# A message-passing layer with a mixture of experts: each quad of the edge stage in three steps, and indices by one transfer per three groups

## What is computed

```python
def gnn(node_feats, ...):
    neigh = segment_sum(node_feats[src], dst, num_segments=n)     # over 200000 edges
    h = (1.0 + eps) * node_feats + neigh
    h = relu(h @ W1 + b1) @ W2 + b2                                # 256 -> 512 -> 256
    return (h - h.mean(0)) * rsqrt(h.var(0) + 1e-5) * gamma + beta # over all nodes

x = x + gnn(layernorm(x), ...)
x = x + ffn(layernorm(x))   # softmax gate, best of 8 experts, capacity 1954 nodes each, 256 -> 1024 -> 256
```

## Time and profile before

| | |
|---|---|
| Timed runs, median of 3 | 2559.24 us (2556.51 to 2567.18) |
| Profiled execution, span | 3175.1 us |
| PE busy | 1826.2 us (58%) |
| DVE busy | 1442.5 us (45%) |
| ACT busy | 694.9 us (22%) |
| POOL busy | 1710.4 us (54%) |
| First to last gather transfer | 118.0 to 2285.7 us |
| Mean granted TensorE clock | 0.777 |

### The profile page before, as it was taken

One profiled execution on the slowest core, in us unless ns is written; L12 is line 12 of the kernel. 1 busy time (PEld: TensorE's weight loads), 2 busy tenths in 40 slices (PEclk: granted clock), 3 DMA queues, 4 the chain that ended last, 5 costly groups with the idle time before them and its releaser, 6 DMA issues. The chain is left out here.

```text
span 3175.1 us, 32785 instructions
## 1 busy us (share of the span) xinstructions
PE 1826.2 (58%) x9046; PEld 1097.7 (35%) x9047; DVE 1442.5 (45%) x4225; ACT 694.9 (22%) x1116; POOL 1710.4 (54%) x1690
## 2 busy tenths in 40 slices
PE   0154444455545455655554455564568768989995
PEld 0022212222222222322222222232357645566664
DVE  8765511543225422531252112122336557786885
ACT  6600000000010001000100001110046554636642
POOL 0366664655645565555644444445315556767874
PEclk9976667676767677777877777777776688999997
DMA  7533354324633354234423332212246432222220
GB/s 244 188 104 106 116 184 138 106 88 132 197 101 91 115 182 148 87 121 144 152 65 121 120 111 65 67 54 79 54 145 216 131 93 75 71 84 73 79 83 18
DMA packets 201521, 361.08 MB, mean 114 GB/s; under 512 B 62117, under 2 KB 125947, under 8 KB 201334
## 3 DMA queue, kind: packets, MB, share of 16 engines
q0 software_dynamic: 69152, 185.00, 19.3%
q1 hardware_dynamic: 130038, 172.60, 16.8%
q10 hardware_dynamic: 2144, 1.05, 0.1%
HBM read 291.08 MB, written 71.92 MB: 114 GB/s over the span
## 5 line engine op out<-in xcount | busy, mean ns | idle before, releaser
L791 POOL DMA_INDIRECT halves<-table,halves x1240 | 1187.7, 958 | 1011.5 <-issue 367.1
L879 PE MATMUL e_sums<-halves 128*128 128x256 f16 x1920 | 334.7, 346 | 392.8 <-issue 244.1
L1062 DVE SCALAR_TENSOR_TENSOR nodes<-e_sums,above,nodes 128x256 f32 (+1 forms) x161 | 77.3, 480 | 967.0 <-remote 437.4
L879 PEld LDWEIGHTS e_sums<-halves 128*128 128x128 f16 x1920 | 229.6, 122 | 508.3 <-issue 425.7
L936 PE MATMUL e_up<-e_hT,W1s 128*128 128x512 f32 (+1 forms) x400 | 229.8, 734 | 234.9 <-ACT e_hT L985 140.2
L985 ACT ACTIVATE e_hT<-e_up 128x1024 f32<-128x1024 f32 (+1 forms) x25 | 25.2, 1007 | 1524.0 <-remote 1185.3
L1720 POOL TENSOR_TENSOR x_midl<-x_midf,x_midh 128x512 f16<-128x512 f32 x200 | 298.7, 1517 | 104.9 <-ACT x_midh L1854 99.4
L917 PE MATMUL e_tally<-w1f,counts 128*128 128x512 f16 x490 | 165.5, 480 | 281.6 <-DMA w1f<-table 204.9
L1126 DVE TENSOR_TENSOR counts<-counts,e_tally 128x490 f32 x220 | 159.8, 726 | 267.8 <-PE e_tally L907 147.9
L1810 PE MATMUL x_down<-halves,x_midh 128*128 128x256 f16 x1472 | 249.4, 277 | 16.6 <-DVE x_yb L1947 15.0
L1786 PE MATMUL x_up<-x_xTh,halves 128*128 128x512 f16 (+1 forms) x800 | 233.6, 371 | 3.1 <-ACT x_midh L1854 3.1
(11 more groups left out here) (208 smaller groups left out, 2752.4 us busy)
## 6 DMA issues: line engine op xcount, KB each, us to landing
w1f<-table SPq DMA_DIRECT2D x120, 512.0 KB
halves<-table,halves POOLq DMA_INDIRECT x1240
slot_rows<-halves SPq DMA_DIRECT2D x64, 268.0 KB
x_row<-slot_rows SPq DMA_DIRECT2D x32, 536.0 KB, 7.4
table<-halves SPq DMA_DIRECT2D x25, 512.0 KB, 2.9
counts<-in_x SPq DMA_DIRECT2D x24, 512.0 KB, 4.5
r_xin<-in_x SPq DMA_DIRECT2D x24, 512.0 KB
out<-r_row SPq DMA_DIRECT2D x24, 512.0 KB
```

Source lines behind the costliest of these rows:

```text
L791: pool.indirect_dma_start(got[:, r, t, :], None, table.rearrange("p h d -> (p h) d"), bass.IndirectOffsetOnAxis(ap=idx[:, r, t:t + 1], axi ...
L879: ins = nc.tensor.matmul(sums[:, place, 0:D], hot[:, place, t, :], got[:, r, t, half * D:(half + 1) * D], start=(t == 0 and half == 0), st ...
```

## The change

Each quad is divided into three steps: the transposes with ACT's copy, the product with W1 with the relus, and the product with W2 with the results. They stand behind three successive groups. A quad starts at its place in `AT`, or where the quad ahead of it has ended: quads 0, 18, 1, 20 and 21 start one or two steps later than before. DVE's measuring comes four steps after the start. In place of its own wait for the results ahead of it, DVE's copy to `hrow` waits until the quad before is through W1, which guards the memory that `hrow` shares with `hT`. The last quad stays whole, behind what is left of quad 23.

The row numbers of an iteration's three groups come by one transfer of 96 bytes per partition, into one of two buffers in turn. Iterations 0 and 1 are loaded at the start. Iteration n+2 is loaded when the three groups of iteration n have landed, behind the pieces of iteration n. POOL waits for indices once per iteration, and its two loops now hold two iterations in their bodies.

The core of the diff:

```diff
+TURN_AT, UP_AT, DOWN_AT, MEASURE_AT = {}, {}, {}, {}
+_slot = 0
+for _q in ORDER[:-1]:
+    _slot = max(_slot, AT[_q][0] * RG + AT[_q][1])
+    TURN_AT[_slot], UP_AT[_slot + 1], DOWN_AT[_slot + 2], MEASURE_AT[_slot + 4] = _q, _q, _q, _q
+    _slot += 3
+STEPS = NIT * RG
+LATE = range(STEPS, max(MEASURE_AT) + 1)
...
-        idx = halves.lend(I32, RG, GT)
+        idx = halves.lend(I32, 2, RG * GT)
...
-                def indices(n, r):
-                    first = n * (RG * GT) + (HT + r * GT)
-                    sp.dma_start(idx[:, r, :], rows_of[:, bass.ds(first, GT)]).then_inc(s_idx[r], 16)
-
-                for r in range(RG):
-                    indices(0, r)
+                def indices(n):
+                    first, width = HT + n * RG * GT, min(RG, NG - n * RG) * GT
+                    sp.dma_start(idx[:, n % 2, 0:width], rows_of[:, first:first + width]).then_inc(s_idx[n % 2], 16)
+
+                indices(0)
+                indices(1)
...
-                def next_indices(n, r):
-                    sp.wait_ge(s_got[r], n * (16 * GT) + 16 * GT)
-                    indices(n + 1, r)
...
                     for r in range(RG):
                         for number in pieces_at(n, r):
                             piece(number)
-                        if (n + 1) * RG + r < NG:
-                            next_indices(n, r)
+                    if n + 2 < NIT:
+                        for r in range(RG):
+                            sp.wait_ge(s_got[r], (n + 1) * (16 * GT))
+                        indices(n + 2)
...
-                with pool.Fori(0, SINGLE // RG):
-                    for r in range(RG):
-                        pool.wait_ge(s_idx[r], have)
-                        pool.wait_ge(s_sum, done)
-                        pool.reg_add(done, done, 1)
-                        gather(r)
-                    pool.reg_add(have, have, 16)
+                with pool.Fori(0, SINGLE // RG // 2):
+                    for h in (1, 0):
+                        pool.wait_ge(s_idx[h], have[h])
+                        pool.reg_add(have[h], have[h], 16)
+                        for r in range(RG):
+                            pool.wait_ge(s_sum, done)
+                            pool.reg_add(done, done, 1)
+                            gather(h, r)
...
                     ins.then_inc(s_turn, 1)
+
+                def product_up(q, width=QN):
+                    k = ORDER.index(q)
                     pe.wait_ge(s_hT, k + 1)
...
                         ins.then_inc(s_up, 1)
+
+                def product_down(q, width=QN):
+                    k = ORDER.index(q)
                     pe.wait_ge(s_mid, k * H1C + H1C)
...
+                def quad_steps(step):
+                    if step in TURN_AT:
+                        turn_rows(TURN_AT[step])
+                    if step in UP_AT:
+                        product_up(UP_AT[step])
+                    if step in DOWN_AT:
+                        product_down(DOWN_AT[step])
...
-                        for q in quads_at(n, r):
-                            quad(q)
-                quad(NQ - 1, LAST)
+                        quad_steps(n * RG + r)
+                for step in LATE:
+                    quad_steps(step)
+                turn_rows(NQ - 1)
+                product_up(NQ - 1, LAST)
+                product_down(NQ - 1, LAST)
...
-                def quad(q, turns):
+                def rows(q, turns):
                     k = ORDER.index(q)
                     if k > 0:
-                        measure(ORDER[k - 1])
+                        dve.wait_ge(s_up, k * H1C)
```

More of the change, by code:

```diff
@@ L989, in quad, with results @@
                                              bias=b1s[:, c:c + 1]).then_inc(s_mid, 1)
+                def results(q, width=QN):
+                    k = ORDER.index(q)
                     act.wait_ge(s_down, k + 1)
@@ L1002, in _ @@
                     for r in range(RG):
-                        for q in quads_at(n, r):
-                            quad(q)
-                quad(NQ - 1, LAST)
+                        quad_steps(n * RG + r)
+                for step in LATE:
+                    quad_steps(step)
+                columns(NQ - 1, LAST)
+                hidden(NQ - 1, LAST)
+                results(NQ - 1, LAST)
             @block.vector
```

62 lines of the change are left out of this document (40 added, 22 removed).

## The result

| | before | after |
|---|---|---|
| Timed, median of the comparison | 2562.71 us (4 runs, 2556.51 to 2567.18) | 2543.75 us (4 runs, 2542.99 to 2545.09) |
| Ratio | 1 | 0.9923, 95% interval 0.9903 to 0.9943 |
| Profiled span | 3175.1 us | 2541.3 us |

The change takes 19 us, 0.8%, where 9 were forecast (2550 of 2559). A second comparison (`after_again` in the table) gave 2547.53 against 2563.52 us, ratio 0.9934 (0.9916 to 0.9951).

What follows compares the result with a forecast made beforehand. The prediction took POOL's gather pace as the bound. Its terms, -5 for split quads, -3 for indices and -0.8 for the tail, sum to -8.8 us on 2559.2, so 2550 us, with a range of 2500 to 2572.

Steps and rivals of the forecast that it cites:

- The bound: Edge stage: POOL's gathers set the pace, 1240 of them 1.25 us apart, 1550 us, which the change doesn't touch.
- The waits in the timed run: Edge stage: POOL waits at most 14 us when timed, against 644 us in the first trace.
- the balance: Timed 2559.2 us less 118.0 ahead, 843.0 behind the edge stage and 33.9 of tail leaves 1564.3 for 1240 gathers.
- The test named in the prediction: Timed median less 118, 843 and 33 us, over 1240 gathers: 1.25 to 1.26 means that POOL never waits.
- Quads in three steps: Splitting quads on TensorE: lone quads worth 0, the dense ones from step 128 on give -5 us (0 to -15).
- The tightest place: Quads at steps 137, 139, 141: sums 142 done after 66 us, POOL needs them at 68; waits 13 at clock 0.74.
- Indices: Late index transfer behind the quad of step 58: its removal gives -3 us (0 to -10).
- The tail: Behind the last gather: 33.1 us against 33.9, so -0.8 us; the split saves nothing at the end.
- C, the clock: Split products start behind idle time at a lower TensorE clock, dense steps become TensorE-bound: slower, 2588 us; chance 0.12.
- B, an inflated route stage: 54 us of the profiled route stage absent when timed, so POOL waits 68 us; the change removes 54: 2505; chance 0.24.
- A, the trace's waits are real: Edge stage: 409 us of POOL's waits are in the timed run, splitting frees half: 2355 us; chance 0.06.
- same: Whole kernel: timed change within 0.5% (12.8 us), what a measurement can't tell from no change; chance 0.48.

Runs made afterwards that it cites:

- after_again: The changed kernel itself, timed a second time on chip C: 2547.5 us, ratio 0.9934 to the kernel before.
- before_seven_2: The kernel before with seven gather transfers per group in place of eight, TensorE's work the same, on chip C: 2427.4 us, ratio 0.9478.
- split_only: The changed kernel with indices loaded by single groups as in the kernel before, so only the quads are split, on chip A: 2541.5 us, ratio 0.9916.
- small_products: The kernel before with 32 of 512 columns in each product of 23 quads, the rest not multiplied, on chip A: 2527.3 us, ratio 0.9857.
- before_again: The kernel before, unchanged, profiled a second time and timed against itself on chip A: 2562.5 us, ratio 0.9999, span 2553.9 us.
- index_only: The kernel before with whole quads but the new index transfers, one per iteration, on chip A: 2560.9 us, ratio 0.9991.
- whole_spaced: The kernel before with whole quads started at the changed kernel's places, at least three steps apart: 3116.6 us (0.9922) on chip B, 2550.1 us (0.9949) on C.
- early_products: The changed kernel with each quad product ahead of its step's sums instead of behind: 2920.1 us (0.9322) on chip B; 2539.6 us (0.9900) on C, as early_products_2.

## Why the prediction was right, and where it wasn't

**The bound: right.** POOL's pace bounds the edge stage. `before_seven_2` takes an eighth of the transfers away and keeps 1.266 us for each; `after`, `split_only` and `small_products` all end at 1564 us of gathers.

**The waits in the timed run: right in size, partly by luck.** At most 14 us were forecast by the balance; the second profile shows 17. The balance had two errors that cancel: the rest behind the edge stage was taken as 843.0 from a disturbed profile and is 816 to 823 undisturbed, and the bare pace was taken as 1.25 us from one group and is 1564.5/1240 = 1.262 over all. The first is 20 to 27 us too much, the second 15 us too little. The test named in the prediction, (2543.75 - 118 - 843 - 33)/1240 = 1.250, reads as "POOL never waits", which is true, but by the same two errors. The pace was there to be read ahead of the result: the first profile's gathers less its 603.6 us of gaps, (2168.6 - 603.6)/1240, are 1.262 too. With that pace and nothing else put right, the balance would have left no wait at all.

**Quads in three steps: the mechanism right, the term too small.** Forecast -5 (0 to -15). Against `before_again` the stretch of the gathers is 18.7 us shorter, of which 17.2 are its waits: 7.4 behind the dense quads (134, 143, 145) where 5 were forecast, 4.0 at group 112 and 1.75 at group 53 where nothing was, and 4.0 for indices at group 62 where 3 were. The tightest place was named rightly: sums 142 to group 145. But its reckoning put the wait at nothing at the full clock and at 13 us at a granted clock of 0.74, and the trace shows 5.6 us at a granted clock of 0.95 (below). From the landing of group 137 (1524.91) to the end of sums 142 (1598.61) it takes 73.7 us, not 66: the sums of six groups, one of them over two windows, are 15.8 us and not five times 2. The waits for DVE's adding and one-hots, 1.7 and 3.1 us, are about what the prediction had allowed for DVE on its way to `hrow`. So the wait hung on sums that it hadn't counted, and not on the clock. The prediction's reason for taking 5, "the denser the work, the higher the clock", stands there without a row; its own rows 6 and 9 say both (0.74 and 0.85 with TensorE busy 51% and 81%, but 0.68 with 72%). The windows of `before_again` from the landing of group 137 to sums 142, columns as in the earlier trace rows:

```profile
1524.90:1598.60 73.70, 62.26 (x232) 32.95 (x232) 19.45 (x72) 15.12 (x21) 51.37 (x54) 0.95 0.35 99
```

What the step also missed is that places ahead of step 128 count. It reckoned a lone quad of 17 us as covered by 28 us of gathers already under way. That holds for a quad beside sums alone; at group 112 a unit's last pieces stand ahead of the quad and tiles behind it, and the way over DVE came on top: 4.0 us.

**Indices: the place right, the credit wrong.** Forecast -3 at step 62. The wait is there, 4.3 us, and the new transfers remove it, as its row is missing in `index_only`. But alone they are worth nothing measurable, as the time goes to the next late sums, and with the split they add nothing: `split_only` 2541.5, after 2543.8, in two comparisons whose ratios (0.9916 and 0.9923) are the same within their intervals. Terms for waits on one chain can't be added one by one when the next wait on it is only partly independent.

**The tail: the order right, the size not.** -0.8 forecast, -1.6 in the profiles (38.0 to 36.4), but one kernel's own tail varies from 36.4 to 39.2. "The split saves nothing at the end" holds. The landing behind it was read as 1.9 us from one group; it was 4.9 for the last.

**Rivals.** C, the clock: wrong. TensorE's products with W1 took 598 ns each in after and 601 in `before_again`. In the dense part, which begins at 1415 us here, the granted clock was 0.89, most of it at 2.4 GHz; it was 0.92 in `before_again`, so it did fall, but POOL didn't wait for it. The window of after (PE, PEld, DVE, ACT, POOL busy, granted clock, DMA, GB/s), the dense part:

```profile
1415.00:1682.00 267.00, 203.33 (x853) 112.20 (x852) 100.18 (x363) 40.29 (x56) 202.47 (x212) 0.89 0.39 110
```

B, an inflated route stage: its premise held in part, since the rest was 20 to 27 us too long in the first profile, but most of that time wasn't in POOL's waits, which are 17 us and not 68. It was in the pace, 1.262 us for 1.25.

A, the trace's waits are real: wrong for the timed run, but the prediction rejected it for a wrong reason. **The step that failed is the sentence that 616 us "aren't there when nobody records".** On chip B they are there in timed runs: 3128.47 us, with spans 2 us below the times. The first profile (3175.1) goes with B's 3128 and the timed median (2559.2) with A's 2563, so the two probably come from different chips; which chips these were isn't recorded, and this is argued, not shown. On a chip like B the mechanism of A applies: the same idea gives 208 us (0.9322, with the products early; the changed kernel itself was not run there), and of the eleven index waits (122.4 us, 110.3 in `whole_spaced`) only that of the start is left (29.6). The forecast of a span 100 to 300 us shorter fell with that step: the profile of after was taken without stalls, and is 634 us shorter for it.

By the prediction's own chances "same" (within 0.5%) was likelier, 0.48 against 0.40 for faster. The change gave 0.8%, and 2543.8 lies in the part below 2546 that had 0.10.

The Trainium skill (Runtime: NRT & Kernel Launch, "The ~15µs preamble/postamble breakdown") puts a gap of about 6.2 us between a profile's total time and the execution time, the same for every kernel, with the profile the longer. The runs here agree that the two lie close, though not with the size or the side: an execution's own time is 1.7 us above its span from first to last instruction (2929.39 and 2927.7 in `early_products`, 2555.64 and 2553.9 in `before_again`). So the 616 us were no effect of recording, and it was wrong to set the rule aside because of them.

## What to carry to other kernels

If one engine issues work at a fixed pace, take its pace over the whole stretch less its long gaps (1.262 us here), not over one clean group (1.25), and multiply by the count: what the stretch takes beyond that is all that better cover can win. Look for the waits at every place where work of several kinds meets (quad, pieces and tiles), not only where one kind is densest, and expect that removing one wait alone feeds the next. When a profile's span and the timed median differ by far more than runs do among themselves, take a second profile before building on either, and don't put the difference down to recording unless one execution shows both numbers.

## What the hardware showed that was not expected

**Two paces of one program.** The kernel before took 2562.96 and 2563.52 us on chips A and C and 3128.47 on B (17 runs, 3109 to 3160). All runs on B belong to one series, so whether it is the chip or the time at which it ran can't be told. On B what waits for TensorE is let go late at many places of the edge stage, by 8 us in the stall above and by up to 17 us ahead of the products, and the granted clock in the stage is 0.75 against 0.83 for the same program on C. The windows of the edge stage of `early_products`, on B,

```profile
116.40:2090.50 1974.10, 1106.78 (x4378) 579.54 (x4378) 765.31 (x2792) 171.33 (x253) 1190.40 (x1244) 0.75 0.41 125
```

and of `early_products_2`, on C:

```profile
117.70:1714.90 1597.20, 1032.42 (x4378) 571.07 (x4378) 764.58 (x2792) 171.54 (x253) 1189.80 (x1244) 0.83 0.50 155
```

TensorE is busy 74 us more and the stretch is 377 us longer, so most of it is idle time and not slower work. Two rows speak against the lower clock as the cause of the idle time. In the stall shown, TensorE stood still at 2.4 GHz for almost 3 us before the clock fell to 1.2 GHz. The windows of `early_products`, from the matmul at 189.52 to 192.80 and from there to DVE's next instruction:

```profile
189.52:192.80 3.28, 0.38 (x1) 0.09 (x1) 0.00 (x0) 0.00 (x0) 2.67 (x3) 0.97 0.80 256
192.82:197.87 5.05, 0.00 (x0) 0.00 (x0) 0.00 (x0) 0.00 (x0) 2.03 (x3) 0.50 0.30 85
```

And `small_products` on chip A, whose TensorE has little to do, had a granted clock of 0.73 in the edge stage without a single wait of POOL:

```profile
118.00:1715.90 1597.90, 942.98 (x4378) 598.75 (x4378) 762.26 (x2792) 168.27 (x253) 1187.32 (x1244) 0.73 0.51 155
```

Nor did a late load of instructions end the stall: the queues marked "instruction" moved no packet between its two ends. What stops TensorE there stays open.

**What a change is worth depends on the pace.** Splitting, with early products, gives 1.0% on C and 6.8% on B.

**One landing doesn't stand for all.** The prediction took 1.9 us from POOL's last transfer of a group to its sums. In after TensorE waited for the rows of 92 groups, and there it was 1.8 to 5.3 us, with a median of 2.5: 5.0 for group 30, 2.7 for group 150, and 4.9 for the last.
